# Stacked low-rank factors, and the identity turned on TensorE, in the opening of a cross-attention kernel

## The chip, the cores and the metric

One core of one Trainium2 chip. The metric is the device time in microseconds (us) from launch to end. Three runs of the kernel before took 832.13, 832.50 and 833.02 us; the median is 832.5 us.

## The reference

x is [8, 128, 512], the context is [8, 128, 512], and there are 32 heads of 128. The low-rank product `W_a @ W_b` (512 x 16 and 16 x 512) is the part of the feed-forward weights that the change touches.

```python
def xattn(x, ctx, mask, bias, ln_w, w_q, w_k, w_v, w_out):
    n = rmsnorm(x) * ln_w
    q, k, v = n @ w_q.T, ctx @ w_k.T, ctx @ w_v.T            # 32 heads of 128
    s = softmax(where(mask, q @ k.T + bias, -inf))           # [8, 32, 128, 128]
    return x + (where(mask, s, 0) @ v) @ w_out.T
x = x + xattn(layernorm(x), ctx_4096, mask, ...)
W = (NF4_CODE[w_codes] * absmax).reshape(512, 512)
h = layernorm(x)
x = x + h @ W.T + 2.0 * (h @ W_a @ W_b)
```

## The kernel before

**Numbers in two parts.** Nearly every large product is written as three products of a rounded high part and a low remainder (`three`, L1176 and following): ScalarE copies a float32 tile to the 32-bit type fp32r (`x_hi`), an engine subtracts it from the whole (`x_lo`), and TensorE sums hi*hi, lo*hi and hi*lo. In the opening ScalarE makes the high parts (`copy`, L603) and VectorE the low ones (`lo`, L895).

**The order of the work.** Each engine has its program written out by hand, with semaphores between them; no scheduler moves anything. An opening (keys and values of the first heads, x normalised and turned, first queries) is followed by a loop over seven groups of four heads, and then by the last group and the feed-forward part. Scores, probabilities and attention of a head stand between the key, value, query and output products of others.

**The opening**, which the change touches:

- SyncE issues all the loads: the two factors `wa` and `wb` of the low-rank product (16 rows of 512 each, L345 and L346), then the first key weights `k_raw` (L320), four blocks of the context (L349), x, the value weights, the mask and the rest.
- GpSimd sets `minus_half` and makes the identity `ident` (L444 to L447); both count on `const_done`.
- TensorE waits for `const_done`, multiplies the identity by itself `WARM_UP` = 4 times (L1247; the products are read by nobody), waits for the two factors, and multiplies three of the four low-rank tiles (`lora_tile`, L1250: stationary 16 x 128 of `wa`, moving 16 x 512 of `wb`, plain float32). Then it waits for `k_lo_done` and `ctx_lo_done` and runs `first_keys`: four calls of 12 products of 128x512 each. The fourth low-rank tile stands behind them, then `first_values(0)`.
- ScalarE copies one element of `minus_half`, then the high parts of `k_raw` (128x1024) and of the four context blocks (128x1024 each). VectorE makes the low parts of the same five in the same order.
- A float32 product shows as two instructions in the trace, an fp32r product as one.

The low-rank tiles are copied out of PSUM, scaled by 2 and stored in DRAM (`lora_copy`, L362), from where GpSimd's decode adds them to the feed-forward weights much later.

Of the kernel before, what the change touches and what calls it, by code (L numbers as in the profile page):

```python
# [6 lines left out]
P = 128  # L7
B = 8
L = 128
D = 512  # L10
# [11 lines left out]
R = 16  # L22
# [41 lines left out]
EARLY_LORA = 3  # L64
TURN_BEFORE = (5, 7)
FFN_TRANSPOSE_BEFORE = 5
WARM_UP = 4

f32 = mybir.dt.float32
f32r = mybir.dt.float32r  # L70
# [25 lines left out]
def xattn_ffn(nc, x_d, ctx_d, mask_d, lnw_d, q_d, k_d, pos_d, wo_d, wv_d, codes_d, absmax_d, wa_d, wb_d, out_d):  # L96
    lora_d = nc.dram_tensor("lora_dram", (GROUPS, P, SLICE), f32, kind="Internal").ap()
    ffn_d = nc.dram_tensor("ffn_dram", (GROUPS, P, SLICE), f32, kind="Internal").ap()
    with ExitStack() as ctx:
        def sb(name, shape, dt=f32):  # L100
            return ctx.enter_context(nc.sbuf_tensor(name, shape, dt))

        def sem(name):
            return ctx.enter_context(nc.semaphore(name))

        xn_hi = sb("xn_hi", [P, C, T], f32r)
# [5 lines left out]
        v = sb("v", [P, B, G * DH])  # L112
# [27 lines left out]
        ident = sb("ident", [P, P])  # L140
# [20 lines left out]
        def flat_blocks(t):  # L161
            return t.rearrange("p k b c -> p (k b c)")

        def two_tiles(t):
            return [t[:, i * D:(i + 1) * D] for i in range(2)]
# [3 lines left out]
        ctx_sum = [ctx_raw[BLOCK_D], flat(wv_raw[:, 0:2, :]), ctx_raw[BLOCK_C], flat(wv_raw[:, 2:4, :])]  # L169
        lora_stage = [flat(k_raw[:, :, :])[:, i * D:(i + 1) * D] for i in range(2)] + [v[:, b, :] for b in (6, 7)]  # L170
        lora_stage = [t.rearrange("p (a b) -> p a b", a=2) for t in lora_stage]
        wa, wb = (v[0:R, i, :] for i in range(2))
        x_stage = [wv_raw[:, i, :] for i in range(4)] + two_tiles(flat_blocks(pT[:, :, :, :])) + [v[:, b, :] for b in (4, 5)]
        ffn_stage = [kT[:, i, f * D:(f + 1) * D] for i in range(2) for f in range(2)]
        mask_raw = codes[:, :].bitcast(u8).rearrange("p (b k) -> p b k", b=B)
# [5 lines left out]
        def ffn_weights(t, c):  # L181
            return t[:, c // 2, c % 2, :]
# [20 lines left out]
        w_ps = [ctx.enter_context(nc.psum_tensor(f"w_ps{i}", [P, D], f32)) for i in range(3)]  # L203
        o_ps = [ctx.enter_context(nc.psum_tensor(f"o_ps{i}", [P, D], f32)) for i in range(3)]

        def s_flat(i):
            return s_ps[i][:, :, :].rearrange("p b k -> p (b k)")
# [18 lines left out]
        lora_banks = [s_flat(1), s_flat(0), o_ps[0][:, :], o_ps[1][:, :]]  # L226
# [2 lines left out]
        x_loaded = [sem(f"x_loaded{i}") for i in range(2)]  # L229
        mask_loaded = sem("mask_loaded")  # L230
        lnw_loaded = sem("lnw_loaded")
        lora_loaded = sem("lora_loaded")
        lora_stored = sem("lora_stored")
        q_loaded = sem("q_loaded")
        k_loaded = sem("k_loaded")
# [28 lines left out]
        lora_done = sem("lora_done")  # L264
# [50 lines left out]
        def _(sp):  # L315
# [3 lines left out]
            def load_k(m):  # L319
                sp.dma_start(k_raw[:, :, :], k_d[m]).then_inc(k_loaded, 16)  # L320
# [21 lines left out]
                        sp.dma_start(pT[Q * k:Q * (k + 1), i, :, :],  # L342
                                     p_blocks[Q * i:Q * (i + 1), k, :, :]).then_inc(pT_loaded, 16)

            sp.dma_start(wa, wa_d).then_inc(lora_loaded, 16)  # L345
            sp.dma_start(wb, wb_d).then_inc(lora_loaded, 16)  # L346
            load_k(0)
            for block_at in range(4):
                sp.dma_start(ctx_raw[block_at], ctx_d[block_at]).then_inc(ctx_loaded[block_at], 16)  # L349
# [89 lines left out]
        def _(pool):  # L439
            def passed(s, value):  # L440
                pool.wait_ge(s, value)
                pool.sem_inc(pool_passed, 1)

            pool.memset(minus_half[:, :], -0.5).then_inc(const_done, 1)  # L444
            pool.memset(ident[:, :], 0.0).then_inc(ident_step, 1)
            pool.wait_ge(ident_step, 1)
# [154 lines left out]
        def _(act):  # L601
            def copy(out, in_, **kw):
                return act.activation(out, in_, ACT.Copy, **kw)  # L603
# [119 lines left out]
                    copy(xn_hi[:, c, half(hf)], turn_banks[hf][c], scale=lnw[:, c:c + 1]).then_inc(xn_hi_done, 1)  # L723


            act.wait_ge(const_done, 2)
            copy(rms_b[:, 0:1], minus_half[:, 0:1])
            act.wait_ge(k_loaded, 16)
            copy(first_hi, k_raw[:, :, :]).then_inc(k_hi_done, PRODUCTS)
            for n in range(4):  # L730
# [162 lines left out]
        def _(dve):  # L893
            def lo(out, whole, hi):
                return dve.tensor_tensor(out, whole, hi.bitcast(f32), ALU.subtract)  # L895
# [134 lines left out]
            def split_ffn(c):  # L1030
                dve.wait_ge(ffn_hi_done, c + 1)
                lo(ffn_weights(ctx_lo, c), wv_raw[:, c, :], ffn_weights(ctx_hi, c)).then_inc(ffn_lo_done, 1)


            dve.wait_ge(k_hi_done, PRODUCTS)
            lo(first_lo, k_raw[:, :, :], first_hi).then_inc(k_lo_done, PRODUCTS)
# [140 lines left out]
        def _(pe):  # L1177
# [67 lines left out]
            pe.wait_ge(const_done, 2)  # L1245
            for _ in range(WARM_UP):
                pe.matmul(w_ps[0][:, 0:P], ident[:, :], ident[:, :], start=True, stop=True)  # L1247

            def lora_tile(c):
                pe.matmul(lora_banks[c], wa[:, c * P:(c + 1) * P], wb, start=True, stop=True).then_inc(lora_done, 1)  # L1250

            def first_keys(head, hf, last=False, parts=1):

# [34 lines left out]
                    t.then_inc(x_turned, 1)  # L1288


            pe.wait_ge(lora_loaded, 32)
            for c in range(EARLY_LORA):
                lora_tile(c)
            pe.wait_ge(k_lo_done, PRODUCTS)
            pe.wait_ge(ctx_lo_done, 1)
            first_keys(1, 0, parts=2)
# [6 lines left out]
            for c in range(EARLY_LORA, C):  # L1303
                lora_tile(c)
# [202 lines left out]
```

## Time and profile before

| | |
|---|---|
| median of three runs | 832.5 us |
| the profiled execution, its own time | 831.71 us |
| its span in the trace | 829.9 us |
| TensorE busy | 99% of the span, 4702 matmuls |
| VectorE, ScalarE, GpSimd busy | 54%, 54%, 65% |
| DMA | 64.46 MB, mean 78 GB/s |

The span runs from the first to the last instruction in the trace; 1.8 us of the execution's own time lie around it. A row of the timeline has the start, the length, the engine, the line and the tiles out<-in; "SPq" is SyncE's queue issuing a DMA. TensorE's instructions overlap, so the distance between two starts tells the rate, not the length of one. The chain that ended last is followed back from the last instruction through whatever released each step.

### The profile page before, as it was taken

How to read it: one execution, taken by the hardware profiler on the slowest of the kernel's cores; microseconds unless marked ns; L12 is line 12 of the kernel's file. 1: busy time of each engine (PE TensorE's matmuls, PEld its weight loads, DVE VectorE, ACT ScalarE, POOL GpSimd, SP SyncE). 2: the span in 40 equal slices, each digit the busy share in tenths (PEclk: the TensorE clock that was granted, in tenths of full speed). 3: DMA queues.
4: the chain of work that ended last, by engine and by line, in shares of the span. 5: the costliest groups of instructions: out<-in, count | busy, mean ns of one | idle time of the engine just before them, and what ended most of it. 6: DMA issues, size and time to landing. Idle time of an engine off the chain costs nothing.

```text
span 829.9 us, 15761 instructions
## 1 busy us (share of the span) xinstructions
PE 824.1 (99%) x4702; PEld 720.3 (87%) x4702; DVE 447.5 (54%) x754; ACT 445.6 (54%) x1297; POOL 535.3 (65%) x556
## 2 busy tenths in 40 slices
PE   9999999999999999999999999999999999999998
PEld 6888888988899888988889888998889888898886
DVE  5785655355634656245553556346562455636683
ACT  5766474464726555364644647355553646447632
POOL 0576778467875778756785578757787567855440
PEclk9999999999999999999999999999999999999999
DMA  8212332122211323113221222113230232311102
GB/s 326 90 42 90 107 94 68 54 92 66 93 36 58 98 68 97 26 69 98 79 89 54 92 66 92 38 55 97 69 96 24 71 98 68 104 41 51 46 13 89
DMA packets 50357, 64.46 MB, mean 78 GB/s; under 512 B 10752, under 2 KB 36480, under 8 KB 49312
## 3 DMA queue, kind: packets, MB, share of 16 engines
q1 hardware_dynamic: 50336, 64.20, 24.9%
q8 instruction: 10, 0.16, 0.1%
q14 instruction: 11, 0.09, 0.0%
HBM read 44.24 MB, written 4.19 MB: 58 GB/s over the span
## 4 chain that ended last, share of the span: by engine, by line
PE 94%; DVE 2%; ACT 2%; SPq 1%; DMA 0%; issue 0%; POOL 0%; POOLq 0%; ACTq 0%
PE w_ps L1184 44%; PE o_ps L1184 35%; PE s_ps L1220 6%; PE s_ps L1226 6%; SPq L342 1%; ACT p_blocks L652 1%; DVE stats L901 1%; DVE resid L1017 1%; PE s_ps L1184 1%; ACT p_blocks L603 1%; PE s_ps L1250 0%; PE o_ps L1250 0%; PE w_ps L1286 0%; PE w_ps L1241 0%; PE w_ps L1247 0%; DMA pT<-p_blocks 0%
## 5 line engine op out<-in xcount | busy, mean ns | idle before, releaser
L531 POOL TENSOR_SCALAR picked<-codes 128x256 f32<-128x256 int32 x112 | 124.3, 1110 | 19.2 <-POOL level L534 15.6
L496 POOL TENSOR_TENSOR p<-pos_raw,mask_add 128x1024 f32<-128x1024 f32 x32 | 69.6, 2175 | 103.1 <-ACT p_blocks L652 102.8
L652 ACT ACTIVATE p_blocks<-p,neg_max 128x128 f32<-128x128 f32 x248 | 96.1, 389 | 48.4 <-DVE neg_max L994 44.0
L534 POOL TENSOR_TENSOR level<-level,picked 128x256 f32<-128x256 f32 x112 | 90.6, 809 | 20.9 <-POOL picked L531 20.9
L468 POOL TENSOR_TENSOR ring_lo<-k_raw,ring_hi 128x256 fp32r<-128x256 f32 x105 | 76.5, 740 | 30.2 <-ACT ring_hi L603 27.3
L603 ACT ACTIVATE ring_hi<-k_raw 128x256 fp32r<-128x256 f32 x105 | 38.8, 414 | 101.0 <-POOL k_raw L458 101.0
L1017 DVE TENSOR_TENSOR resid<-o_ps,resid 128x512 f32<-128x512 f32 x102 | 68.7, 686 | 44.7 <-PE o_ps L1184 44.5
L1184 PE MATMUL w_ps<-ctx_hi,ring_hi 128*128 128x512 f32 x210 | 84.7, 403 | 0.0
L1184 PE MATMUL w_ps<-ctx_hi,ring_lo 128*128 128x512 f32 x210 | 82.1, 391 | 0.0
L1184 PE MATMUL w_ps<-ctx_lo,ring_hi 128*128 128x512 f32 x210 | 81.7, 389 | 0.0
L603 ACT ACTIVATE p_blocks<-p_blocks,row_scale 128x128 f32<-128x128 f32 x248 | 77.2, 391 | 1.1 <-DVE row_scale L1001 1.1
L1184 PE MATMUL o_ps<-wo_hi,attn_hi 128*128 128x512 f32 x180 | 70.2, 390 | 0.0
L1184 PE MATMUL o_ps<-wo_hi,attn_lo 128*128 128x512 f32 x180 | 70.1, 389 | 0.0
L1184 PE MATMUL o_ps<-wo_lo,attn_hi 128*128 128x512 f32 x180 | 70.0, 389 | 0.0
L992 DVE TENSOR_TENSOR p<-s_ps,p 128x512 f32<-128x512 f32 x62 | 42.5, 686 | 41.8 <-PE s_ps L1220 41.8
L1220 PEld LDWEIGHTS s_ps<-kT,qT 128*128 128x128 f32 x496 | 59.8, 191 | 1.9
L1220 PE MATMUL s_ps<-kT,qT 128*128 128x128 f32 x496 | 60.4, 275 | 0.0
L1226 PEld LDWEIGHTS s_ps<-pT,v 128*128 128x128 f32 x480 | 58.2, 191 | 2.3
L1009 DVE STREAM_TRANSPOSE p_blocks<-p_blocks 128x512 f32<-128x512 f32 x60 | 39.1, 691 | 36.7 <-ACT p_blocks L603 36.7
L1226 PE MATMUL s_ps<-pT,v 128*128 128x128 f32 x480 | 58.4, 275 | 0.0
L895 DVE TENSOR_TENSOR attn_lo<-s_ps,attn_hi 128x512 fp32r<-128x512 f32 x62 | 40.9, 680 | 31.1 <-ACT attn_hi L603 31.1
L984 DVE TENSOR_TENSOR v<-w_ps,v 128x512 f32<-128x512 f32 x21 | 14.5, 692 | 76.7 <-PE w_ps L1184 76.7
(229 smaller groups left out, 2289.8 us busy)
## 6 DMA issues: line engine op xcount, KB each, us to landing
pT<-p_blocks SPq DMA_DIRECT2D x480, 32.0 KB, 1.8
k_raw<-k_dram SPq DMA_DIRECT2D x16, 512.0 KB, 3.5
wv_raw<-wv_dram SPq DMA_DIRECT2D x8, 1024.0 KB, 4.8
q_raw<-q_dram SPq DMA_DIRECT2D x32, 256.0 KB, 3.7
wo_raw<-wo_dram SPq DMA_DIRECT2D x32, 256.0 KB, 4.0
resid<-x_dram SPq DMA_DIRECT2D x2, 1024.0 KB, 12.6
pos_raw<-pos_dram SPq DMA_DIRECT2D x32, 64.0 KB, 3.8
out_dram<-resid SPq DMA_DIRECT2D x8, 256.0 KB, 2.0
```

What stands on the lines that cost most here:

```text
L468: return pool.tensor_tensor(out, whole, hi.bitcast(f32), ALU.subtract)
L496: pool.tensor_tensor(p[:, :, :], pos, mask_add[:, :, :], ALU.add).then_inc(bias_done, 1)
L531: then(pool.tensor_scalar((level if code == 0 else picked)[:, :], codes[:, :], float(code), NF4[code], match, ALU.mult))
L534: then(pool.tensor_tensor(level[:, :], level[:, :], picked[:, :], ALU.add))
L603: return act.activation(out, in_, ACT.Copy, **kw)
L652: e = act.activation(out(b), p[:, b, :].rearrange("p (k c) -> p k c", c=Q), ACT.Exp, bias=neg_max[:, b:b + 1], accum_out=prob_sum[:, b:b + 1])
L895: return dve.tensor_tensor(out, whole, hi.bitcast(f32), ALU.subtract)
L992: dve.tensor_tensor(p[:, bs, :], banks[hf][:, :, :], p[:, bs, :], ALU.add).then_inc(biased, 1)
L1017: dve.tensor_tensor(resid[:, b, :], bank, resid[:, b, :], ALU.add).then_inc(out_added, 1)
L1184: mm = pe.matmul(out, l, r, start=opens and i == 0, stop=closes and i == n - 1, skip_group_check=True)
L1220: s = pe.matmul(banks[hf][:, i, :], qT[:, at], kT[:, slot, at], start=True, stop=True)
L1226: o = pe.matmul(out[:, i * L:(i + 1) * L], v[:, b, j * DH:(j + 1) * DH], by_keys(b), start=True, stop=True)
```

## The change

The two factors get 96 partitions instead of 16: three copies of each, 32 partitions apart, with zeros between. GpSimd clears both tiles first, and ScalarE waits for that and then issues six loads itself (three of `wa`, three of `wb`). ScalarE copies both 96x512 tiles to fp32r; VectorE replaces rows 64 to 95 of the copy of `wa`, and rows 32 to 63 of that of `wb`, by the low remainders. One fp32r product over 96 rows then is hi*hi + hi*lo + lo*hi: the sum that `three` makes with three instructions. SyncE no longer loads the factors. The identity is multiplied 27 times ahead of the low-rank tiles, not 4, and 5 times between them and the first keys.

```diff
--- before.py
+++ after.py
@@ -64,7 +64,11 @@
 EARLY_LORA = 3
 TURN_BEFORE = (5, 7)
 FFN_TRANSPOSE_BEFORE = 5
-WARM_UP = 4
+WARM_UP = 27
+STAY_WARM = 5
+
+STACKED = 3
+STACK = 32
 
 f32 = mybir.dt.float32
 f32r = mybir.dt.float32r
@@ -169,7 +173,9 @@
         ctx_sum = [ctx_raw[BLOCK_D], flat(wv_raw[:, 0:2, :]), ctx_raw[BLOCK_C], flat(wv_raw[:, 2:4, :])]
         lora_stage = [flat(k_raw[:, :, :])[:, i * D:(i + 1) * D] for i in range(2)] + [v[:, b, :] for b in (6, 7)]
         lora_stage = [t.rearrange("p (a b) -> p a b", a=2) for t in lora_stage]
-        wa, wb = (v[0:R, i, :] for i in range(2))
+        wa, wb = (v[0:STACKED * STACK, i, :] for i in range(2))
+        wa_parts, wb_parts = (xn_hi[0:STACKED * STACK, i, 0:D] for i in range(2))
+        wa_low, wb_low = slice(2 * STACK, 3 * STACK), slice(STACK, 2 * STACK)
         x_stage = [wv_raw[:, i, :] for i in range(4)] + two_tiles(flat_blocks(pT[:, :, :, :])) + [v[:, b, :] for b in (4, 5)]
         ffn_stage = [kT[:, i, f * D:(f + 1) * D] for i in range(2) for f in range(2)]
         mask_raw = codes[:, :].bitcast(u8).rearrange("p (b k) -> p b k", b=B)
@@ -229,7 +235,10 @@
         x_loaded = [sem(f"x_loaded{i}") for i in range(2)]
         mask_loaded = sem("mask_loaded")
         lnw_loaded = sem("lnw_loaded")
+        lora_cleared = sem("lora_cleared")
         lora_loaded = sem("lora_loaded")
+        lora_hi_done = sem("lora_hi_done")
+        lora_lo_done = sem("lora_lo_done")
         lora_stored = sem("lora_stored")
         q_loaded = sem("q_loaded")
         k_loaded = sem("k_loaded")
@@ -342,8 +351,6 @@
                         sp.dma_start(pT[Q * k:Q * (k + 1), i, :, :],
                                      p_blocks[Q * i:Q * (i + 1), k, :, :]).then_inc(pT_loaded, 16)
 
-            sp.dma_start(wa, wa_d).then_inc(lora_loaded, 16)
-            sp.dma_start(wb, wb_d).then_inc(lora_loaded, 16)
             load_k(0)
             for block_at in range(4):
                 sp.dma_start(ctx_raw[block_at], ctx_d[block_at]).then_inc(ctx_loaded[block_at], 16)
@@ -441,6 +448,8 @@
                 pool.wait_ge(s, value)
                 pool.sem_inc(pool_passed, 1)
 
+            for factor in (wa, wb):
+                pool.memset(factor, 0.0).then_inc(lora_cleared, 1)
             pool.memset(minus_half[:, :], -0.5).then_inc(const_done, 1)
             pool.memset(ident[:, :], 0.0).then_inc(ident_step, 1)
             pool.wait_ge(ident_step, 1)
@@ -723,8 +732,16 @@
                     copy(xn_hi[:, c, half(hf)], turn_banks[hf][c], scale=lnw[:, c:c + 1]).then_inc(xn_hi_done, 1)
 
 
+            act.wait_ge(lora_cleared, 2)
+            for i in range(STACKED):
+                act.dma_start(wa[STACK * i:STACK * i + R, :], wa_d).then_inc(lora_loaded, 16)
+                act.dma_start(wb[STACK * i:STACK * i + R, :], wb_d).then_inc(lora_loaded, 16)
+
             act.wait_ge(const_done, 2)
             copy(rms_b[:, 0:1], minus_half[:, 0:1])
+            act.wait_ge(lora_loaded, 32 * STACKED)
+            copy(wa_parts, wa).then_inc(lora_hi_done, 1)
+            copy(wb_parts, wb).then_inc(lora_hi_done, 1)
             act.wait_ge(k_loaded, 16)
             copy(first_hi, k_raw[:, :, :]).then_inc(k_hi_done, PRODUCTS)
             for n in range(4):
@@ -1031,6 +1048,9 @@
                 dve.wait_ge(ffn_hi_done, c + 1)
                 lo(ffn_weights(ctx_lo, c), wv_raw[:, c, :], ffn_weights(ctx_hi, c)).then_inc(ffn_lo_done, 1)
 
+            for n, (parts, whole, rows) in enumerate(((wa_parts, wa, wa_low), (wb_parts, wb, wb_low))):
+                dve.wait_ge(lora_hi_done, n + 1)
+                lo(parts[rows, :], whole[rows, :], parts[rows, :]).then_inc(lora_lo_done, 1)
 
             dve.wait_ge(k_hi_done, PRODUCTS)
             lo(first_lo, k_raw[:, :, :], first_hi).then_inc(k_lo_done, PRODUCTS)
@@ -1247,7 +1267,7 @@
                 pe.matmul(w_ps[0][:, 0:P], ident[:, :], ident[:, :], start=True, stop=True)
 
             def lora_tile(c):
-                pe.matmul(lora_banks[c], wa[:, c * P:(c + 1) * P], wb, start=True, stop=True).then_inc(lora_done, 1)
+                pe.matmul(lora_banks[c], wa_parts[:, c * P:(c + 1) * P], wb_parts, start=True, stop=True).then_inc(lora_done, 1)
 
             def first_keys(head, hf, last=False, parts=1):
 
@@ -1288,9 +1308,11 @@
                     t.then_inc(x_turned, 1)
 
 
-            pe.wait_ge(lora_loaded, 32)
+            pe.wait_ge(lora_lo_done, 2)
             for c in range(EARLY_LORA):
                 lora_tile(c)
+            for _ in range(STAY_WARM):
+                pe.matmul(w_ps[0][:, 0:P], ident[:, :], ident[:, :], start=True, stop=True)
             pe.wait_ge(k_lo_done, PRODUCTS)
             pe.wait_ge(ctx_lo_done, 1)
             first_keys(1, 0, parts=2)
```

ScalarE's queue, first rows before (`v` holds `wa` and `wb`; `attn_hi<-k_raw` is the first key weights' high part, `ctx_hi<-qT` the first context block's):

```order
L603 ACT_TABLE_LOAD
L603 ACTIVATE rms_b<-minus_half 128x1 [waits const_done]
L603 ACTIVATE attn_hi<-k_raw 128x1024 [waits k_loaded]
L603 ACTIVATE ctx_hi<-qT 128x1024 [waits ctx_loaded0]
L603 ACTIVATE ctx_hi<-p 128x1024 [waits ctx_loaded1]
```

and now:

```order
L737 DMA v<-wa_dram 16x512 [waits lora_cleared]
L738 DMA v<-wb_dram 16x512
L737 DMA v<-wa_dram 16x512
L738 DMA v<-wb_dram 16x512
L737 DMA v<-wa_dram 16x512
L738 DMA v<-wb_dram 16x512
L612 ACT_TABLE_LOAD
L612 ACTIVATE rms_b<-minus_half 128x1 [waits const_done]
L612 ACTIVATE xn_hi<-v 96x512 [waits lora_loaded]
L612 ACTIVATE xn_hi<-v 96x512
L612 ACTIVATE attn_hi<-k_raw 128x1024 [waits k_loaded]
L612 ACTIVATE ctx_hi<-qT 128x1024 [waits ctx_loaded0]
```

Six DMA issues and a table load stand first, and two copies that wait for the loads stand ahead of the copy of `k_raw`.

TensorE's queue, from its first instruction to the first keys, before:

```order
L1247 MATMUL w_ps<-ident 128x128 [waits const_done]
L1247 MATMUL w_ps<-ident 128x128 x3
L1250 MATMUL s_ps<-v 128x512 [waits lora_loaded]
L1250 MATMUL s_ps<-v 128x512
L1250 MATMUL o_ps<-v 128x512
L1184 MATMUL w_ps<-ctx_hi,attn_hi 128x512 [waits ctx_lo_done,k_lo_done]
L1184 MATMUL w_ps<-ctx_lo,attn_hi 128x512
```

and now (`xn_hi` holds the stacked parts):

```order
L1267 MATMUL w_ps<-ident 128x128 [waits const_done]
L1267 MATMUL w_ps<-ident 128x128 x26
L1270 MATMUL s_ps<-xn_hi 128x512 [waits lora_lo_done]
L1270 MATMUL s_ps<-xn_hi 128x512
L1270 MATMUL o_ps<-xn_hi 128x512
L1315 MATMUL w_ps<-ident 128x128 x5
L1204 MATMUL w_ps<-ctx_hi,attn_hi 128x512 [waits ctx_lo_done,k_lo_done]
L1204 MATMUL w_ps<-ctx_lo,attn_hi 128x512
```

The low-rank tiles wait for VectorE's `lora_lo_done` in place of the loads, with 23 more identity products ahead of them and 5 behind.

GpSimd's queue ahead of the identity, now:

```order
L445 UNCONDITIONAL_BRANCH [waits barrier_Pool_Activation_PE_DVE_SP_gather]
L452 MEMSET v 96x512 x2
L453 MEMSET minus_half 128x8
L454 MEMSET ident 128x128
L456 ISA [waits ident_step]
L456 AFFINE_SELECT ident<-ident 128x128
```

Before, `minus_half` was the first of these; the two memsets of 96x512 are new, and the identity stands behind them.

## Rows read from the trace of the kernel before

**Rows 1.** Page of the kernel before: engine totals; shares of the chain that ended last

```profile
PE 824.1 (99%) x4702; PEld 720.3 (87%) x4702; DVE 447.5 (54%) x754; ACT 445.6 (54%) x1297; POOL 535.3 (65%) x556
...
PE 94%; DVE 2%; ACT 2%; SPq 1%; DMA 0%; issue 0%; POOL 0%; POOLq 0%; ACTq 0%
```

**Rows 2.** Waits of TensorE over the whole span: engine, line, releaser: us, times, longest

```profile
PE w_ps L1247 <- POOL ident L447: 1.6, 1, 1.6
PE o_ps L1220 <- ACT qT L603: 0.7, 1, 0.7
PE o_ps L1184 <- DVE xn_lo L895: 0.4, 1, 0.4
```

**Rows 3.** Chain that ended last, from 1.5 us on: start us, us, what

```profile
1.57 2.07 PE w_ps L1247 x8
3.65 3.71 PE s_ps L1250 x4
...
9.06 10.44 PE w_ps L1184 x36
19.50 2.72 PE s_ps L1184 x12
22.21 1.05 PE o_ps L1250 x2
23.27 8.39 PE o_ps L1184 x36
31.65 1.31 PE w_ps L1286 x12
```

**Rows 4.** Timeline, TensorE's products of the first keys: start us, us, what

```profile
12.57 0.63 PE L1184 MATMUL w_ps<-ctx_hi,attn_lo 128*128 128x512 f32 x1
...
13.00 0.56 PE L1184 MATMUL w_ps<-ctx_hi,attn_hi 128*128 128x512 f32 x1
...
13.39 0.39 PE L1184 MATMUL w_ps<-ctx_lo,attn_hi 128*128 128x512 f32 x1
...
13.63 0.39 PE L1184 MATMUL w_ps<-ctx_hi,attn_lo 128*128 128x512 f32 x1
```

**Rows 5.** Stretch 9.00 to 13.33, TensorE: us, PE busy (count), granted clock, DMA

```profile
9.00:13.33 4.33, 4.33 (x11) 1.00 1.05 414
```

**Rows 6.** Timeline of the other engines in the opening

```profile
0.73 0.40 SPq L345 DMA_DIRECT2D v<-wa_dram  x1
0.73 1.28 ACT L603 ACT_TABLE_LOAD   x1 [0.73 <-PEq L1500]
0.73 0.10 POOL L444 MEMSET minus_half<- 128x8 f32 x1 [0.29 <-POOLq L1500]
0.77 0.20 POOL L445 MEMSET ident<- 128x128 f32 x1
...
1.19 0.40 SPq L346 DMA_DIRECT2D v<-wb_dram  x1
1.22 0.29 POOL L447 TENSOR_SCALAR_AFFINE_SELECT ident<-ident 128x128 f32<-128x128 f32 x1 [0.25 <-POOL ident L445]
...
5.15 1.06 ACT L603 ACTIVATE attn_hi<-k_raw 128x1024 fp32r<-128x1024 f32 x1 [2.92 <-DMA k_raw<-k_dram]
...
6.31 1.23 DVE L895 TENSOR_TENSOR attn_lo<-k_raw,attn_hi 128x1024 fp32r<-128x1024 f32 x1 [5.44 <-ACT attn_hi L603]
6.41 1.06 ACT L603 ACTIVATE ctx_hi<-qT 128x1024 fp32r<-128x1024 f32 x1 [0.21 <-DMA qT<-ctx_dram]
...
7.50 1.23 DVE L895 TENSOR_TENSOR ctx_lo<-qT,ctx_hi 128x1024 fp32r<-128x1024 f32 x1
...
21.02 0.63 ACT L603 ACTIVATE q_hi<-q_raw 128x512 fp32r<-128x512 f32 x1 [0.89 <-DMA q_raw<-q_dram]
```

**Rows 7.** DMA issues: what, queue, count, KB, median us to landing

```profile
v<-wa_dram SPq DMA_DIRECT2D x1, 32.0 KB, 1.9
...
lnw<-lnw_dram SPq DMA_DIRECT2D x1, 2.0 KB, 11.5
```

## The prediction

> **What bounds the kernel now.** I read the page first: TensorE is busy for 99% of the span, and the chain that ended last is TensorE for 94% of it [rows 1]. Then the waits: over the whole span TensorE waits three times, and 1.6 us of the 2.7 are the wait for the identity at the very start [rows 2]. So what TensorE does ahead of its first useful product, and at what rate, is passed on to the end, and what other engines do counts only where TensorE comes to wait for it.
>
> The chain then shows the opening piece by piece [rows 3]. Identity from 1.57; low-rank tiles (plain float32, two instructions each of about 0.93 us) from 3.65; 36 products of the first keys from 9.06 and 12 more from 19.50 to 22.2; the fourth low-rank tile, 1.05 us; first values at 23.27. A full-rate product of 128x512 takes 2.72 / 12 = 0.227 us. The timeline shows what the first ones take: starts at 12.57 and 13.00 are 0.43 apart, 13.00 and 13.39 are 0.39 apart, 13.39 and 13.63 are 0.24 apart [rows 4]. 512 columns in 0.43 us are the 1.2 GHz level, in 0.23 us the 2.4 GHz level. The granted clock reads 1.00 all through this stretch [rows 5], so the record misses the change and I go by the distances: TensorE ran low from 1.57 to about 13.3, though it was never idle, and rose 4.3 us after the first keys began. Some ten products of the keys ran low, each 0.2 us too long: about 2.1 us. That is one sum the change could win. The other is the float32 tiles: only the fourth stands behind the keys, 1.05 us for what one fp32r product does in 0.23. The first three lie ahead of the keys, in time in which the keys' operands were not ready: VectorE's low part of the first context block began at 7.50 and took 1.23 [rows 6], so it was there at 8.7, and TensorE began at 9.0.
>
> The most that the change could give is therefore 2.1 + 0.8 = 2.9 us, if the first keys still began at 9.0. They do not, as follows. 0.2% of this kernel is 1.7 us, about what a measurement of it can tell from no change.
>
> **GpSimd: two memsets ahead of the identity.** The memset of 8 elements took 0.10, that of 128 took 0.20 [rows 6]: 0.83 ns an element, so 0.52 us for 512. Starts of short ones are 0.04 apart while each takes 0.10, so some 0.06 of each overlaps: two add 0.9 us. The identity, and with it TensorE's first instruction, moves from 1.57 to 2.5. In itself this idle time costs nothing, since TensorE has nothing to do yet. Bounds: 0.4 us, two memsets like the 128x128 one, and 2 us, twice the slope.
>
> **ScalarE: six issues, then two copies.** ScalarE may issue from 1.7. SyncE's two issues of the same factors begin 0.46 apart [rows 6], so the sixth begins at 1.7 + 5 x 0.46 = 4.0. The table load (1.28), which now stands behind the issues, ends at about 5.7, under the landing. The six carry 192 KB, where the two carried 64. When does the last one land? The first load of the trace took 1.9 us on empty queues; the load of lnw, 2 KB behind a full SyncE queue, took 11.5 [rows 7]. These are the bounds. The new loads go out on ScalarE's own queue, with the 512 KB loads of the keys and context in flight on SyncE's. I take 2.4 us, nearest to the first row, because nothing stands ahead of them in their own queue: landed at 6.4.
>
> The Trainium skill (DMA: Bandwidth & Descriptors, "Issuing engines are not separate DMA queues") says that DMAs from ScalarE and SyncE run on the same 16 engines and interleave, and that a second issuing engine saves issue time alone. By its "Queues, rings and completion order" an engine alternates between the queues packet by packet; by that the loads land near the 1.9 and the sum stands, while by the row of lnw it would be 8 us worse, a rival below. No row of this case has two queues at work.
>
> Behind the landing stand, in a row: two high parts of 96x512, 0.63 each by the copy of 128x512 [rows 6], so 1.2; the high part of k_raw 1.06; its low part on VectorE 1.2; the low part of the first context block 1.23. Together 4.7 us: the keys' operands are ready at 6.4 + 4.7 = 11.1, against 8.7 before. VectorE's two low parts of the factors (at most 0.7 each) run under ScalarE's copy of k_raw and end by 8.3. That k_raw itself is issued 0.9 us earlier, the two factor loads having left SyncE's queue, gives nothing: ScalarE waited 2.9 us for it before [rows 6], and now it waits for the factors. The later context blocks are no limit: each follows 1.2 us behind the last on VectorE, while TensorE takes 1.4 us over the first half of a call and 2.7 over the next.
>
> **TensorE: 27 identities, three tiles, five identities.** An identity is two instructions. At the full rate 12 turns of 128 columns took 1.31 us [rows 3], 0.109 each; at the low rate twice that, 0.218 (the row of the 8 gives 0.26 each with its first fill and last drain). When does the clock rise? Before, identities ran for 2 us and the 16-row tiles for 5.4, and it did not rise; 4.3 us of 128-row products did it. The identity is a 128-row product, so I count the same 4.3 us from its start: 2.5 + 4.3 = 6.8. Bounds: at once, and never by identities. With a rise at 6.8, 20 of the 54 instructions run low and 34 at 0.109 take 3.7 us: the identities end at 10.5. Three fp32r tiles add 0.7, the five further identities 1.1: **the first keys begin at 12.3**, not at 11.1. TensorE, kept busy by instructions that nobody reads, is late for its operands by 1.2 us. That is where most of the gain goes.
>
> **The sum.** 48 products at 0.227 take 10.9: 23.2. The fourth tile 0.23: first values at 23.4, against 23.27 before. **+0.2 us.** In terms: first keys 3.3 us later, 2.3 us less for them (13.2 to 10.9), 0.8 us less for the fourth tile. From there on nothing is changed and every later step moves with TensorE: stagings, turns and drains follow its products. The profiled execution took 831.7 us with a span of 829.9; the new span is 830.1. The median of the runs is 0.8 above the profiled one, so the predicted median is 832.5 + 0.2 = 832.7.
>
> In general the change costs the start of the first keys less 12.1 us, and that start is the later of two: 11.1, which is the landing plus 4.7; and half of the time of the rise plus 8.9 (54 identities, each microsecond of low clock costing half).
>
> **Rivals.**
>
> *The identity does not raise the clock (slower).* For it: 2 us of identities before left no mark, and plain float32 products ran for 7.4 us without a rise. Nothing tells whether it was their 16 rows or their form that failed to. Then 54 instructions at 0.218 end at 14.2, tiles at 0.43 at 15.5, five more identities at 17.7; ten keys run low as before (4.3), 38 at 0.227 take 8.6, with the fourth tile 30.9. That is +7.6: 840.1 us. It decides from a rise later than 9.8, which makes over 1.7 us. Against it: the array is filled by 128 rows in both kinds.
>
> *The factor loads land late (slower).* Only from 3.6 us after the last issue do they matter; by lnw's 11.5 the keys begin at 4.0 + 11.5 + 4.7 = 20.2, +8.1 us: 840.6; halfway between the bounds, 6.7, it is +3.3, 835.8. For it: the 16 DMA engines are then busy with the keys and the context (a share of 1.05 in [rows 5], a little later). Against it: an own queue, small loads.
>
> *Rise and loads are both early (faster).* With a rise below 4.4 the operands decide: 11.1, and -1.0 us, not to be told from no change. With landing at 5.9 and copies of 0.5 us the keys begin at 10.4, -1.7 us: 830.8. It needs a rise almost at TensorE's first instruction.
>
> **How the numbers follow.** Forecast (a rise between 4.4 and 9.8, operands by 13.8, so -1.0 to +1.7): 0.65. No rise by identities: 0.13. Loads late enough to tell: 0.11. Early on both: 0.11. So faster 0.11, same 0.64, slower 0.25, with 0.01 of the forecast's edge put to slower. The range leaves out the two far ends: it goes from 830.9 (the forecast's own low end is 831.5, and the faster rival is at the edge) to 836.0, which takes in the halfway case of late loads; it leaves out the missing rise and the far case of lnw.
>
> **What would show it.** TensorE's first identity at 2.5; starts of the identities at twice the distance until about 6.8; their end at 10.5 with lora_lo_done long past; the first keys at 12.3 with all starts 0.23 apart; first values at 23.4; no new wait of TensorE. Wrong, if the identities stand 0.2 apart to their end, if TensorE waits for VectorE at the tiles or the first keys, or if the last factor load takes over 3.6 us.

## The result, and the profile after

The changed kernel takes 836.7 us (median of 6 runs, 835.3 to 838.1), the kernel before 832.6 in the same series (831.9 to 833.2): a ratio of 1.005, 95% interval 1.0038 to 1.0063. It is slower by 4.1 us, beyond the range's upper end of 836.0. The profiled execution took 836.66 us, with a span of 834.8. That span is 4.9 us over the one before and the medians are 4.1 apart: the profiled execution before (831.71 us) was 0.9 us faster than its median.

The page: the busy totals hardly move, the chain that ended last has a load in it, and there is one queue more.

```profile
PE 826.2 (99%) x4754; PEld 727.0 (87%) x4754; DVE 447.1 (54%) x756; ACT 446.1 (53%) x1299; POOL 537.0 (64%) x558
...
q10 hardware_dynamic: 192, 0.20, 0.1%
...
PE 95%; DVE 2%; ACT 1%; DMA 1%; ACTq 0%; issue 0%; POOL 0%; DVEq 0%; POOLq 0%
```

TensorE's busy time is 2.1 us more than before [rows 1], the span 4.9 us. The shares of the chain now have 1% for DMA, which is one load. The waits of TensorE, as in [rows 2]:

```profile
PE w_ps L1267 <- POOL ident L456: 2.5, 1, 2.5
PE s_ps L1270 <- DVE xn_hi L912: 2.0, 1, 2.0
PE o_ps L1240 <- ACT qT L612: 0.4, 1, 0.4
```

Ahead of the low-rank tiles stands a new wait of 2.0 us on VectorE's parts of the factors. The chain shows what is behind it, where [rows 3] had TensorE alone from 1.57 on (start us, us, what):

```profile
0.73 0.99 POOL v L452 x2
...
4.18 7.22 DMA v<-wb_dram
...
11.96 0.61 ACT xn_hi L612
12.57 0.96 ACT attn_hi L612
...
14.86 1.15 DVE ctx_lo L912
...
16.14 9.59 PE w_ps L1204 x36
25.73 2.72 PE s_ps L1204 x12
...
28.68 8.18 PE o_ps L1204 x36
```

GpSimd's clearing, ScalarE's six issues, 7.2 us for the last load to land, then two copies, the high and the low part of k_raw, and the low part of the first context block (its high part runs beside VectorE). The first keys begin at 16.1 (before: 9.0), the first values at 28.7 (before: 23.3, [rows 3]), 5.4 us later. Of these 0.5 come back further on: the first 36 products of the values take 8.18 us in place of 8.39, and the later wait for `qT` is 0.4 us in place of 0.7 [rows 2]. That leaves the 4.9 of the span.

The keys themselves do not all run at the full rate. TensorE's starts at the head of the first keys (timeline; the columns are those of [rows 4]):

```profile
16.70 0.63 PE L1204 MATMUL w_ps<-ctx_lo,attn_hi 128*128 128x512 f32 x1
...
17.13 0.63 PE L1204 MATMUL w_ps<-ctx_hi,attn_lo 128*128 128x512 f32 x1
...
18.72 0.39 PE L1204 MATMUL w_ps<-ctx_hi,attn_hi 128*128 128x512 f32 x1
...
18.95 0.40 PE L1204 MATMUL w_ps<-ctx_lo,attn_hi 128*128 128x512 f32 x1
```

From 16.70 to 17.13 are 0.43 us, the lower level; from 18.72 to 18.95, 0.23. This time the record has the fall of the clock; ahead of its first entry it reads 1.00 whatever the rate, so for the rise the counts of instructions stand. The same execution in stretches, TensorE alone (us, busy and count, granted clock, DMA share, GB/s):

```profile
6.00:8.00 2.00, 2.00 (x12) 1.00 1.05 332
8.00:10.00 2.00, 2.00 (x18) 1.00 1.01 292
...
11.50:13.50 2.00, 0.05 (x1) 1.00 1.07 398
...
14.30:16.00 1.70, 1.62 (x11) 0.75 0.97 398
16.10:18.50 2.40, 2.36 (x6) 0.50 1.03 383
```

The identities run 12 in 2 us until about 8 (the lower level), then 18 in 2 us: they did raise the clock, 5.7 us after the first of them. Then TensorE stood still for 2.0 us; the granted clock fell within the stretch from 14.30 to 16.00, with identities running again, and is at 0.50 up to 18.5. What landed when:

```profile
v<-wa_dram ACTq DMA_DIRECT2D x3, 32.0 KB, 6.1
v<-wb_dram ACTq DMA_DIRECT2D x3, 32.0 KB, 6.3
```

The factor loads took a median of 6.1 and 6.3 us (5.5 to 7.2 each); the two loads before took 1.9 and 1.8.

The packets of the two queues tell more. From 1.7 to 4.5 us the engines ran 253 packets of SyncE's queue and none of ScalarE's; from 7 to 8 us, 65 and 46. ScalarE's first load was issued at 1.74, and no packet of its queue ran before 4.9; the last ran at 10.8. So part of the delay lies ahead of the first packet, and the rest is spent between SyncE's packets.

### The profile page after: what moved, and what is told of

It reads as the page before. It is cut to its first block, busy times and chain, and to the rows that moved or that the text cites. A ratio compares the mean times of both kernels' runs of the same rounds, so it can differ in the third digit from the quotient of the medians.

```text
span 834.8 us, 15875 instructions
## 1 busy us (share of the span) xinstructions
PE 826.2 (99%) x4754; PEld 727.0 (87%) x4754; DVE 447.1 (54%) x756; ACT 446.1 (53%) x1299; POOL 537.0 (64%) x558
## 4 chain that ended last, share of the span: by engine, by line
PE 95%; DVE 2%; ACT 1%; DMA 1%; ACTq 0%; issue 0%; POOL 0%; DVEq 0%; POOLq 0%
PE w_ps L1204 45%; PE o_ps L1204 35%; PE s_ps L1240 7%; PE s_ps L1246 6%; DMA v<-wb_dram 1%; DVE stats L918 1%; DVE resid L1034 1%; PE s_ps L1204 1%; ACT p_blocks L661 0%; PE w_ps L1306 0%; ACT p_blocks L612 0%; PE w_ps L1261 0%; ACT attn_hi L612 0%; PE w_ps L1246 0%; DVE ctx_lo L912 0%
```

## The experiments

The theory after the result: (1) the factors land late because ScalarE issues their loads while SyncE's 512 KB loads are in flight; (2) since the change puts the factors ahead of k_raw on ScalarE and VectorE, each microsecond of that is one of the first keys; (3) the gap that it leaves on TensorE lowers the clock. The rivals: six small loads are slow by themselves; the identities delay or fail to warm; ScalarE's issues slow SyncE's loads. Each run's time stands beside runs of the kernel before on the same chip (832.3, 832.4 and 832.0 us in the three series).

### Are the loads slow by themselves?

```diff
+            sp.wait_ge(lora_loaded, 32 * STACKED)
             load_k(0)
```

> The change, with SyncE's first load held until the six factor loads have landed. Theory A (the factor loads are late because SyncE's 512 KB loads are in flight on the same 16 DMA engines): the factor loads land 1.9 to 2.5 us after their issue instead of 5.5 to 7.2, the last one by about 6.5 us of the span. Theory B (six loads of 16 rows on ScalarE's queue are slow by themselves): they still take 5 us or more. The keys' weights then come about 5 us later, so the total says little; A gives a time near or below the change's 836.7 all the same, as the first keys begin near 6.5 + 4.0 (landing of k_raw and the first context block) + 3.5 = 14 to 15.

Measured: 833.8 us (one run). The loads, and the chain of waits:

```profile
v<-wa_dram ACTq DMA_DIRECT2D x3, 32.0 KB, 1.8
v<-wb_dram ACTq DMA_DIRECT2D x3, 32.0 KB, 1.8
```

```profile
4.06 1.78 DMA v<-wb_dram
```

On the same queue, in the same shape and number, the loads land in 1.8 us once nothing else is in flight. The late landing in the change is contention, not the queue by itself or the 16 rows. And the kernel that holds SyncE back by 5 us was 3 us faster than the change in this one run. The first keys begin at 13.05, a microsecond earlier than expected; TensorE then waits 0.6 us for the second context block, and the first values begin at 25.3, so the kernel is no faster than the one before.

### The same six loads, issued by SyncE

```diff
-            act.wait_ge(lora_cleared, 2)
-            for i in range(STACKED):
-                act.dma_start(wa[STACK * i:STACK * i + R, :], wa_d).then_inc(lora_loaded, 16)
-                act.dma_start(wb[STACK * i:STACK * i + R, :], wb_d).then_inc(lora_loaded, 16)
...
+            sp.wait_ge(lora_cleared, 2)
+            for i in range(STACKED):
+                sp.dma_start(wa[STACK * i:STACK * i + R, :], wa_d).then_inc(lora_loaded, 16)
+                sp.dma_start(wb[STACK * i:STACK * i + R, :], wb_d).then_inc(lora_loaded, 16)
             load_k(0)
```

> The change, with the same six loads issued by SyncE ahead of its own, as the two stood before; still behind GpSimd's clearing. Theory A (contention with loads that are ahead of them in time): landed by 6.5 us, first keys at about 12 us (k_raw is issued at 4.5 and lands near 8, so the context block becomes the limit), first values near 23.5, 832.7 +- 0.8 us. Theory B (the small 16-row loads are slow by themselves, whoever issues): landed near 11, 836 us or more.

Measured: 832.95 us (10 runs, 832.1 to 833.6), ratio 1.0005 (0.9996 to 1.0015). Its chain of waits is TensorE alone from the identity on:

```profile
2.50 8.97 PE w_ps L1266 x54
...
13.29 8.20 PE w_ps L1203 x36
...
24.44 8.18 PE o_ps L1203 x36
```

The factors land 1.8 us after their issues, the operands of the keys are ready at 11.7, and TensorE comes to the keys at 13.0 to 13.3, behind its identities. All starts are then 0.23 us apart. This is the kernel that the prediction described, with no change in time that can be told. But its first keys begin at 13.0 in place of 12.3 and its first values at 24.4 in place of 23.4, since the identities ran low until 8.2. Who issues the six loads, and with it that they go out ahead of the large ones (k_raw is issued at 4.5 here, at 0.7 in the change), is worth 3.8 us against the 836.7 (3.4 when each is taken against the kernel before in its own series).

### Was the gap the cause of the lower clock?

```diff
-WARM_UP = 27
-STAY_WARM = 5
+WARM_UP = 37
+STAY_WARM = 8
```

> The change, with 37 identities ahead of the low-rank tiles and 8 behind them, so that TensorE has no gap before the first keys. Theory A (the clock fell because of the 2 us gap): all starts of the first keys are 0.23 us apart, the first keys begin within 0.5 us of where they do in the change, and the time is 1.2 to 2.0 us below the change's 836.7: near 835. Theory B (identities do not hold the clock, the rise and the fall have another cause): the first keys still run at 0.43 us each for 2 us and more, and the time is that of the change.

Measured: 835.57 us (5 runs, 834.9 to 835.8), ratio 1.0039 (1.0025 to 1.0054). Chain of waits:

```profile
13.17 0.54 PE s_ps L1270 x2
...
15.73 8.27 PE w_ps L1204 x36
24.00 2.72 PE s_ps L1204 x12
```

No gap, and the 36 + 12 products of the keys take 8.27 + 2.72 = 11.0 us, in place of 9.59 + 2.72 = 12.3 in the change. That is 1.3 us. Loads and keys are as late as before, within 0.5 us (first keys at 15.7). The medians are 1.15 us apart, just under what theory A gave, and 0.8 when each is taken against the kernel before in its own series; the intervals overlap, so the size rests on the profiles. The mean granted clock of each run says the same: of the six runs of the change the one at 835.3 us reads 1.000, the five from 836.1 to 838.1 read 0.998 down to 0.995, and all five runs here read 1.000. Theory 3 holds for the change, and the fall did not come in every execution of it.

### The identities alone

```diff
-WARM_UP = 4
+WARM_UP = 27
```

in the kernel before, and nothing else.

> The kernel before, with 27 identities instead of 4 and nothing else. Theory A (the identity raises the clock as any product of 128 rows does): the identities run at 0.21 us an instruction until some 5 to 7 us after the first and at 0.11 after that, end near 10.5, the float32 tiles take about 0.5 us a piece as long as the clock stays up, and the first keys begin near 14: total 833.5 to 836. Whether the 16-row tiles hold the clock shows in the starts of the first keys: 0.23 apart if they do, 0.43 if it falls. Theory B (identities have no part in it): identities at 0.21 to their end at 13, first keys near 18, 840 us.

Measured: 835.62 us (5 runs, 835.4 to 836.0), ratio 1.0041 (1.0026 to 1.0055). The chain and, below it, TensorE in two stretches (us, busy and count, granted clock, DMA share, GB/s):

```profile
1.57 8.87 PE w_ps L1247 x54
10.44 1.91 PE s_ps L1250 x4
...
13.20 10.02 PE w_ps L1184 x36
```

```profile
13.00:13.80 0.80, 0.80 (x4) 1.00 1.16 486
13.80:14.50 0.70, 0.70 (x4) 0.51 0.92 386
```

54 instructions in 8.87 us: the identities raise the clock here too. Then the three float32 tiles of 16 rows run at the full rate (0.46 us an instruction, in place of 0.90), but shortly after them, at about 13.8, the granted clock falls to 0.5: the first keys still start at the full rate, those from 14.0 on are 0.43 apart, and 48 products take 12.7 us. All five runs have a mean granted clock of 0.997 or 0.998; those of the kernel before in the series have 0.999 or 1.000. TensorE had not stood still at all; the 2.8 us of tiles of 16 rows are what lay ahead of the fall, as 5.4 us of them lay ahead of the low clock at 9 us in the kernel before. Of the two readings that the prediction left open, the rows or the float32 form, the form is out: the identities are float32 too. The 512 columns of a tile are out as well, since the keys have as many; the 16 rows are what is left, though no run changed them alone. The 27 identities did not cure the slow keys of the kernel before while its float32 tiles stand between; other numbers of them were not tried.

### The stacked parts alone

```diff
-WARM_UP = 27
-STAY_WARM = 5
+WARM_UP = 4
+STAY_WARM = 0
```

> The change with 4 identities ahead of the low-rank tiles and none behind, so only the stacked parts and their loads by ScalarE are left. TensorE stands still from about 4.3 us until the tiles. Theory A (the late landing of the factors sets the first keys, the identities only set the clock): the first keys begin where they do in the change, near 16, and run at 0.43 us a product for at least 3.4 us: 0.5 to 1.5 us over the change, 837 to 838.5. Theory B (the many identities delay the tiles or the keys): below the change's 836.7.

Measured: 838.41 us (4 runs, 838.0 to 839.7), ratio 1.0079 (1.0063 to 1.0094). TensorE's waits:

```profile
PE s_ps L1270 <- DVE xn_hi L912: 8.5, 1, 8.5
...
PE w_ps L1204 <- DVE ctx_lo L912: 1.0, 1, 1.0
PE o_ps L1240 <- ACT qT L612: 0.9, 1, 0.9
PE o_ps L1204 <- DVE attn_lo L912: 0.7, 1, 0.7
```

TensorE stands still for 8.5 us and 1.0 us, and the first keys begin at 15.7, as in the change within 0.5 us: the identities delay nothing there. The median is 1.7 us above the change's, and the stacked parts and their loads alone cost 6.0 us. But in the profiled execution those 1.7 us did not arise in the opening. The first values begin at 28.6, as in the change (28.7): the last load landed 0.4 us earlier, and the 48 products took 12.7 us in place of 12.3. The difference between the two profiles comes later, in a wait for `attn_lo` at 96 us that the change does not have and in a longer wait for `qT` in the last group. What the identities bring to the opening by their clock is thus 0.4 us here; why the two later waits are there stays open.

### The factors taken off the way of the keys

ScalarE and VectorE split the factors behind the four context blocks, TensorE runs the three tiles between the second and the third call of the first keys, GpSimd clears behind the identity, 16 identities.

```diff
...
             first_keys(0, 0)
+            pe.wait_ge(lora_lo_done, 2)
+            for c in range(EARLY_LORA):
+                lora_tile(c)
             pe.wait_ge(ctx_lo_done, 3)
...
```

> The change with the factors taken off the way of the keys, their loads unchanged in kind: ScalarE splits the factors behind the four context blocks, VectorE too, TensorE runs the three low-rank tiles between the second and the third call of the first keys, the clearing stands behind the identity, ScalarE's table load ahead of its issues, and 16 identities stand ahead of the first keys. Theory A (what costs is that everything waits for the factors): the loads still take 5 to 7 us to land, and nobody notices; first keys at 8.7 to 9.5, some of them still at 0.43 us, first values at 21 to 22.5: 830.2 to 832, below the kernel before (832.3). Theory B (ScalarE's issues slow down SyncE's loads, and the keys come late in any case): first keys after 10.5, 832.5 or more.

Measured: 832.36 us (11 runs, 831.9 to 833.8), ratio 1.0000 (0.9991 to 1.0009): as the kernel before, 4.4 us under the change, above what theory A gave. The loads land in 6.2 to 6.4 us as ever. The keys begin at 10.15, not at 9:

```profile
5.29 1.08 ACTq L739 DMA_DIRECT2D v<-wb_dram  x1
...
6.48 1.06 ACT L611 ACTIVATE attn_hi<-k_raw 128x1024 fp32r<-128x1024 f32 x1 [4.25 <-issue]
...
10.15 0.47 PE L1201 MATMUL w_ps<-ctx_hi,attn_hi 128*128 128x512 f32 x1 [3.13 <-DVE ctx_lo L910]
...
10.46 0.39 PE L1201 MATMUL w_ps<-ctx_lo,attn_hi 128*128 128x512 f32 x1
...
10.69 0.40 PE L1201 MATMUL w_ps<-ctx_hi,attn_lo 128*128 128x512 f32 x1
...
12.96 1.06 ACT L611 ACTIVATE ctx_hi<-wo_raw 128x1024 fp32r<-128x1024 f32 x1 [0.93 <-DMA wo_raw<-ctx_dram]
```

Issuing the six loads keeps ScalarE until 6.4, and it splits k_raw only at 6.5; the last context block is split at 12.96, where it was at 11.6 before, although it was issued 0.9 us earlier: it took 10.3 us to land, in place of 8.1. A part of that is the earlier issue; with the same issue time and nothing on ScalarE's queue (the last run below) it took 8.9. So both theories had a part: being behind the factors is the large cost, and ScalarE's loads do slow SyncE's.

TensorE stood still for 3.1 us ahead of these keys, longer than in the change, and yet their starts are 0.23 apart from the second on: the clock held. A gap alone does not decide that it falls.

### Each factor as one load

The stacked tiles with their zeros are laid out in DRAM ahead of the launch, in time that the metric does not count, so one load of 96 rows (192 KB) brings each, and nothing is cleared.

```diff
-            for factor in (wa, wb):
-                pool.memset(factor, 0.0).then_inc(lora_cleared, 1)
...
+            sp.dma_start(wa, wa_d).then_inc(lora_loaded, 16)
+            sp.dma_start(wb, wb_d).then_inc(lora_loaded, 16)
             load_k(0)
...
-        "wa_dram": np.asarray(L0_ffn_W_a).T,
-        "wb_dram": np.asarray(L0_ffn_W_b),
+        "wa_dram": stacked(np.asarray(L0_ffn_W_a).T),
+        "wb_dram": stacked(np.asarray(L0_ffn_W_b)),
```

> The change with each factor already stacked with its zeros in DRAM, so that one load of 96 rows brings it, with no clearing and no six issues; SyncE issues the two loads ahead of the keys' weights as before, 9 identities stand ahead of the tiles and 5 behind. Theory A (early landing frees the rest): factors landed by 3.5, their parts made while ScalarE and VectorE wait for k_raw, first keys at 8.8 to 9.5 with the clock up or rising within 2 us, first values near 20.5 to 21.5: 829.5 to 831.3. Theory B (the rest of the gain is lost to the clock, since tiles of 96 rows between identities do not hold it): first keys on time but at 0.43 us for 3 us or more: 832 or more.

> As the last one, but ScalarE issues the two loads, ahead of its table load. Theory A (the time to land is set by how much of SyncE's loads is in flight at the issue): issued at 0.7 and 1.2, beside the keys' weights alone, they land 2 to 3.5 us after it, by 4.5, and the first keys begin at 9 or before, since k_raw is issued 0.9 us earlier: within 0.7 us of the last one. Theory B (a load on ScalarE's queue is served behind SyncE's): 5 us or more to land, first keys after 11, 832 or more.

Measured, SyncE issuing: 831.32 us (11 runs, 830.9 to 833.0), ratio 0.9997 (0.9988 to 1.0006), not told from the kernel before. Its runs stand in two groups, seven from 830.9 to 832.0 and four from 832.6 to 833.0. Measured, ScalarE issuing: 834.35 us (11 runs, 832.8 to 834.8), ratio 1.0022 (1.0013 to 1.0031). The landings, first of the one and then of the other:

```profile
v<-wa_dram SPq DMA_DIRECT2D x1, 192.0 KB, 2.6
v<-wb_dram SPq DMA_DIRECT2D x1, 192.0 KB, 2.8
```

```profile
v<-wa_dram ACTq DMA_DIRECT2D x1, 192.0 KB, 4.3
v<-wb_dram ACTq DMA_DIRECT2D x1, 192.0 KB, 6.3
```

Two loads alike, issued at the same times, 0.7 and 1.2 us, land after 2.6 and 2.8 us on SyncE's queue, ahead of its large loads, and after 4.3 and 6.3 us on ScalarE's, beside them. Of the second, theory B is right in its price (over 832, landings up to 6.3 us), though the first of the two loads came earlier than it said: issuing early is no help while the other queue goes on issuing. The first keys begin at 13.2 there, at 10.9 here. The profile there is of the fastest of the eleven runs. In it TensorE waits 3.8 us for the factors and the clock is low from 9.9 to 13.3; six of the seven runs from 834.3 to 834.8 have a mean granted clock of 0.995 or 0.996, below its 0.998, so a part of the 3 us between the two kernels is the clock and not the landing.

With SyncE issuing, the factors landed at 4.0 and not by 3.5, and k_raw is now the late one: the 384 KB ahead of it move it to 7.2, and TensorE waits 2.5 us behind its five identities. Hence first keys at 10.9 and not at 8.8 to 9.5, and first values at 22.3: theory A has the time to within 0.1 us, but not its steps. Theory B is out for this execution, whose keys all start 0.23 apart.

### That gap filled

```diff
-WARM_UP = 9
-STAY_WARM = 5
+WARM_UP = 11
+STAY_WARM = 13
```

> The kernel with whole stacked factors loaded first by SyncE (831.3 us, its runs in two clusters, 830.9 to 832.0 and 832.6 to 833.0), with 11 identities ahead of the tiles and 13 behind them instead of 9 and 5, so that the gap of 2.5 us ahead of the first keys is filled. Theory A (the upper cluster is the clock that fell over the gap): first keys still near 10.9, mean clock 1.00 in every run, no run over 832, median 830.9 to 831.3. Theory B (the clusters come from something else, the loads for one): both clusters stay.

Measured: 830.81 us (11 runs, 830.6 to 831.5), ratio 0.9986 (0.9977 to 0.9995). The upper group of runs is gone and no run is over 831.5, as theory A has it. That the clock made that group is argued: of its four runs one has a mean granted clock of 0.998 and three of 0.999, and none was profiled. The wait ahead of the first keys is 0.7 us in place of 2.5. They begin at 11.4, half a microsecond later than without, since k_raw landed later; but this profile is of the slowest of the eleven runs. The median is 0.5 us lower, and by no more than 0.1 us when each is taken against the kernel before in its own series (1.2 us under it in place of 1.1).

### Whole factors, loaded behind the context blocks

Whole factors as in the last two sections, loaded by SyncE behind the context blocks and split there too, tiles between the second and the third call, 20 identities ahead of the first keys and none behind.

```diff
-WARM_UP = 27
-STAY_WARM = 5
+WARM_UP = 20
...
             for block_at in range(4):
                 sp.dma_start(ctx_raw[block_at], ctx_d[block_at]).then_inc(ctx_loaded[block_at], 16)
+            sp.dma_start(wa, wa_d).then_inc(lora_loaded, 16)
+            sp.dma_start(wb, wb_d).then_inc(lora_loaded, 16)
...
             first_keys(0, 0)
+            pe.wait_ge(lora_lo_done, 2)
+            for c in range(EARLY_LORA):
+                lora_tile(c)
             pe.wait_ge(ctx_lo_done, 3)
...
```

> Each factor stacked with its zeros in DRAM and loaded by SyncE behind the four context blocks; ScalarE and VectorE split it behind those blocks, TensorE runs the three tiles between the second and the third call of the first keys; 20 identities fill TensorE's time from 1.6 us to about 9. Theory A (two terms made the change slow, the factors' place ahead of the keys and the gap; without both the clock and the fourth tile are won): k_raw lands near 4.3, first keys at 9 to 9.5, all at 0.23 us a product from about there, no gap of over 1 us, first values at 20.5 to 21.5: 829.8 to 831, below the kernel before by more than its interval. Theory B (the bytes of the context bound the keys, and what is won is waited for again): first values at 22.5 or later, 831.5 or more.

Measured: 830.49 us (11 runs, 829.4 to 831.3), ratio to the kernel before 0.9979 (0.9970 to 0.9988), 1.5 us faster, and 6.2 us faster than the change. Chain and waits:

```profile
15.31 0.73 PE s_ps L1262 x2
...
21.95 8.18 PE o_ps L1196 x36
```

```profile
PE s_ps L1262 <- DVE xn_hi L905: 0.9, 1, 0.9
...
PE w_ps L1196 <- DVE ctx_lo L905: 0.6, 2, 0.5
```

First values at 21.95, 1.3 us ahead of the kernel before; 1.5 us are still waited, 0.9 of it for the factors' low parts. This is theory A in its time, but the first values are half a microsecond outside what it said, and the first keys, at 7.9, a microsecond earlier than it said. The factor loads took 7.5 and 9.3 us here, behind the context in the same queue, and 0.9 us is all that TensorE waited for them.

## Why the prediction was wrong

It named the mechanism that came, as a rival at 11%, and gave its forecast to the wrong landing. Step by step:

- **GpSimd's memsets, ScalarE's issues.** Right. The two memsets took 0.98 us (0.9 said), the identity's first product stands at 2.49 (2.5), the sixth issue at 4.18 (4.0), the table load ends at 6.0, under the landing.
- **"I take 2.4 us, nearest to the first row, because nothing stands ahead of them in their own queue."** This is the step that failed. The last load took 7.2 us. Between the bounds of 1.9 and 11.5 [rows 7] the lower row was wrongly chosen: it is not enough that nothing stands ahead in the own queue, what the other queue has in flight counts too. The load of [rows 7] that took 1.9 us had empty engines; ahead of the last of the new ones SyncE has issued 2.5 MB of key weights and context and 2 MB of x and value weights. With the new loads on empty engines it is 1.8; with SyncE issuing them first, 1.8 as well.
- **The rule beside it.** The Trainium skill (DMA: Bandwidth & Descriptors, "Issuing engines are not separate DMA queues") says that the issuing engines share the 16 DMA engines and interleave. The runs agree: 1.8 us alone, 6.1 and 6.3 beside SyncE's loads. What I drew from its "Queues, rings and completion order", that a small load alternating packet by packet with large ones lands near the 1.9, the runs contradict. Packets of both queues do run in the same microsecond (46 of ScalarE's and 65 of SyncE's from 7 to 8 us), but the first of ScalarE's came 3.2 us after the first issue, in place of 1.0 with SyncE idle, and the landings took 4 us and more longer.
- **From landing to keys: 4.7 us.** Right: 11.40 to 16.14.
- **The rise of the clock by identities.** Right in kind. It came 5.7 us after the first identity, not 4.3, so they ended at 11.5 and not at 10.5. But 4.3 was one execution's value: the starts of the identities turn from 0.21 to 0.11 apart anywhere from 3.1 us (the last run) and 3.4 (keys first) to 5.6 (SyncE issuing) after the first one, and in the run with the gap filled the clock rose 6.0 us after it. A single number for the rise could hit or miss by luck. In the run in which SyncE issues, where this decides, the keys begin at 13.0 against the 12.3 forecast, which is what the prediction's own formula gives for that rise (half of 8.2, plus 8.9), and the time is 832.95 against the 832.7.
- **"The start of the first keys less 12.1 us".** It gives 16.1 - 12.1 = 4.0 us for the late landing, and the first values are 5.4 late. The other 1.4 is the clock: a late landing leaves TensorE without work, and I priced no loss for that. The 48 products took 12.3 us in place of 10.9. Filling the gap gave 1.3 us back. That 4.0 us is so near the 4.1 between the medians is in part luck: the profiles are 4.9 apart, with the 1.4 of the clock in them and 0.5 that came back later.
- **The fourth tile.** Right: 0.23 us in place of 1.05.
- **No new wait of TensorE.** Wrong, 2.0 us for the parts of the factors; it was named as what would refute the forecast, as was a landing over 3.6 us.
- **The late loads as a rival.** Its mechanism is what came, and its halfway case (835.8) is 0.9 us under the measured time; with the 7.2 us that were measured the same sum gives 836.5.

What stays open: how the DMA engines share out between the two queues. The runs show the landings for a few orders of issue, not the rule behind them, and not why ScalarE's first packet came so late; nor did I try the six loads by ScalarE behind the context blocks' landing.

## What to carry to other kernels

Here a small load that something early waits for belongs ahead of the large ones in their own queue (1.8 us to land); a second issuing engine gave it no right of way (5.5 to 7.2 us). Price a load by the traffic in flight when it is issued, and ask which chain it is put on: the low-rank product was needed by nobody for a long time, and the change hung the first keys on it. Idle time of TensorE ahead of a bound stretch can cost twice: here 1.4 us of clock came on top of the wait, in most executions but not in all, so price both with the second as a chance. And a sum from one profile should stand beside the spread of the runs: landings and the rise of the clock moved by one to three microseconds between profiles.

## What was not expected of the hardware

- With no gap on TensorE at all, the raised clock fell within a microsecond behind 2.8 us of 16-row products, in the run with the identities alone. Identity products, nearly all of whose factors are zeros, raised it, 5.7 us after the first in the change and 3.1 to 5.6 in others.
- In the change TensorE stood still from 11.5 to 13.5 and the clock fell at about 15.1, with TensorE at work again; it was back at 18.6. With the keys first TensorE stood still for 3.1 us, and with whole factors by SyncE for 2.5, and the clock did not fall in those profiles.
- Two loads issued at the same moments land after 2.6 and 2.8 us on the queue that issues the large ones behind them, and after 4.3 and 6.3 us on the other queue.
- Six small loads on ScalarE's queue slowed SyncE's: the third context block, issued at 2.1 us, took 7.9 to 9.0 us to land in the four kernels that have them (9.0 in the change), against 6.8 in the last run, which issues it at the same moment and has nothing on ScalarE's queue.
